# Low halves of q and k made by GpSimd from a float32 copy, in an attention and mixture-of-experts kernel

## The chip, the cores and the metric

One core of one Trainium2 chip runs the whole program. The metric is the device time in microseconds. The engines are TensorE (PE; its weight loads PEld), VectorE (DVE), ScalarE (ACT), GpSimd (POOL) and SyncE (SP), which issues most transfers. Matmul results lie in PSUM banks of 128 x 512 float32; the rest lies in SBUF.

## The reference

```python
# x: (16, 512, 256); 16 heads of 16; 8 experts of 512, two for each token
qkv = layernorm(x) @ W_attn + b_attn
q, k = rope(q), rope(k)                  # angles by head index
att  = softmax(causal(q @ k.T / 4))
x    = x + (att @ v) @ W_proj + b_proj
xf   = layernorm(x)
w    = top2(softmax((layernorm(xf) * ln_scale + ln_bias) @ gate_w.T))   # renormalised
x    = x + swiglu(xf, sWg, sWu, sWd) + sum_e w[:, e] * swiglu(xf, Wg[e], Wu[e], Wd[e])
```

## The kernel before

The program has an attention stage (to about 860 us), then the shared expert with the routing, then the routed experts. The change touches the attention stage alone.

Attention works on 16 batches of 512 tokens. A batch is a pass of `body(b, ...)`, and each engine runs its own copy of it: four groups `g` of four heads, and in each group five units `s`. A place (g, s) is called a slot here. In each slot TensorE makes the scores of one unit (`scores`, L1675, with the mask L1695), VectorE takes their row maxima (`row_max`), and TensorE may write the next scores only when the maxima are taken. Three slots into the next group the scores are made again with the row maxima subtracted (`shifted`, L1723), ScalarE takes the exponential (`exponentials`, L884), GpSimd clears what is above the diagonal (`select`, L702), and TensorE multiplies with v (`mix`, L1749). The maxima reach the operand as rows: `maxima` transposes them on TensorE (L1709, s = 0), ScalarE copies them to `m_row` (L893, s = 1), SyncE moves four rows into `q_op` (`load_shift`, L480, s = 2), and `shifted` of unit 0 (s = 3) waits for them.

All other work is placed by hand: constants name the slot of each step, and every engine does its steps in order of the slots. Beside batch b the projections of batch b + 1 are made, and the output projection and residual of batch b - 1. Float32 precision comes from pairs of halves: three products of a high and a low part stand for one (`products`, L1615).

q and k of the next batch are four blocks `i` of 128 x 512 (0 and 1: q and k of the first eight heads; 2 and 3: of the others). `project_qk(n, i)` writes each into the one bank `ps_q`. Then two engines read the bank:

```python
nc.scalar.activation(qkh[:, i, :], src[:], ACT.Identity, bias=bcol[:, i:i + 1])   # qk_high, L861
nc.vector.scalar_tensor_tensor(out=qkl[:, i, :], in0=src[:], scalar=bcol[:, i:i + 1],
                               in1=qkh[:, i, :], op0=ALU.add, op1=ALU.subtract)   # qk_low, L1077
```

Both results are float16. TensorE uses `ps_q` also for the transposes of the normalised input (`transpose_xn`, L1606) and for v (`project_v`), and it waits for `qkl_done` before three of these: `project_v` of j = 1 in slot (2,1), `project_qk` of i = 3 in (3,1), and the first `transpose_xn` in (0,1) of the next pass.

SyncE stores the halves to memory (`store_qk`, L458) and loads them back in the order of the heads, with high or low parts stacked (`load_qk`, L472, 12 transfers for each j). For j = 0 (blocks 0 and 1) store and first loads are in slot (2,3), and the loads go on to (3,3); for j = 1 the store is in (0,2) of the next pass. SyncE does all of this in one order, with `load_shift`, the loads of x, and `store_half` (L511, L512), which stores the residual rows. A wait of SyncE holds up all that is behind it.

GpSimd adds the bias of the output projection to the residual (`X_BIAS`, L723): one piece in (1,4), three in (3,2).

Of the kernel before, what the change touches and what calls it, by code (L numbers as in the profile page):

```python
# [16 lines left out]
P = 128  # L17
# [27 lines left out]
def build(nc, x, w_attn, b_attn, w_proj, b_proj, ln_scale, ln_bias, gate_w, Wg, Wu, Wd, sWg, sWu, sWd, rope, out):  # L45
# [41 lines left out]
    with ExitStack() as ctx:  # L87
# [9 lines left out]
        def sem(name):  # L97
# [57 lines left out]
        xh = sb_a("xh", [P, 2, T], F32R)  # L155
        xl = sb_a("xl", [P, 2, T], F32R)
        qkh = sb_a("qkh", [P, 4, T], F16)
        qkl = sb_a("qkl", [P, 4, T], F16)
# [89 lines left out]
                 "pool_const attn_w qk_topped biascols scales_done "  # L248
                 "xn_done shift_done xnT_in xh_done xl_done qk_in qkh_done qkl_done v_in v_done "
                 "s_in max_done m_in m_done mrow_in t_in exp_done sel_done pv_in o_done "  # L250
# [26 lines left out]
        XN_T, XN_HIGH, XN_LOW = ((0, 1), (0, 2)), ((0, 1), (0, 2)), ((0, 1), (0, 3))  # L277
        QK, QK_HIGH = ((0, 4), (1, 4), (2, 4), (3, 1)), ((1, 0), (2, 0), (3, 0), (3, 4))
        QK_LOW = ((1, 0), (2, 0), (3, 0), (0, 1))
        V_PROJ, V_PROJ_B, VALUES = ((1, 2), (2, 1)), ((1, 3), (2, 1)), ((1, 3), (2, 3))  # L280
# [6 lines left out]
        PROJ, PROJ_B = ((3, 3), (1, 1)), ((3, 4), (1, 1))  # L287
        X_BIAS = ((1, 4), (3, 2), (3, 2), (3, 2))
        X1, X1_STATS, X1_VARIANCE = ((3, 4), (1, 1)), ((0, 0), (1, 2)), ((0, 4), (2, 4))
# [349 lines left out]
        def _(pool):  # L639
# [42 lines left out]
            input_rstd(1)  # L682

            def residual_rstd(bp, j):
                pool.wait_ge(S["varb_done"], 2 * bp + j + 1)
                pool.sem_inc(S["pool_passed"], 1)
                nc.gpsimd.tensor_tensor(rstdb[:], mvb[:, :, 1], neghalf[:, 0:2],
                                        ALU.pow).then_inc(S["rstdb_done"], 1)
# [17 lines left out]
            def body(b, par, cur, prev, prev2, nxt, nxt2):  # L706
                for g in range(NG):
                    G = 4 * b + g
                    has1 = (cur or g < 1) and (prev or g >= 1)
                    has2 = (cur or g < 2) and (prev or g >= 2)  # L710
                    for s in range(UN):
                        if s >= LAG - UN and has1:
                            select(G - 1, s + UN - LAG, (g - 1) % 2)
                        elif s < LAG - UN and has2:
                            select(G - 2, s + 2 * UN - LAG, g % 2)
                        if prev:
                            for t in range(NT):
# [120 lines left out]
        def _(act):  # L838
# [16 lines left out]

            def qk_high(n, i, src=ps_q):

                act.wait_ge(S["qk_in"], 4 * n + i + 1)
                if some(32 * n):
                    act.wait_ge(qk_stored[i // 2], 32 * n)  # L860
                nc.scalar.activation(qkh[:, i, :], src[:], ACT.Identity,  # L861
                                     bias=bcol[:, i:i + 1]).then_inc(S["qkh_done"], 1)

            def prologue():
# [6 lines left out]
                for i in range(4):  # L871
                    qk_high(0, i, QK_BANK[i])
                for t in range(NT):
# [30 lines left out]
            def body(b, par, cur, prev, prev2, nxt, nxt2):  # L904
                for g in range(NG):
# [3 lines left out]
                    for s in range(UN):  # L909
                        for i in range(4):  # L910
                            if cur and prev and (g, s) == QK_HIGH[i] and QK_HIGH[i] < QK[i]:
                                qk_high(b, i)
                        if s == M_ROWS and has1:
# [16 lines left out]
                        if nxt:  # L930
# [3 lines left out]
                            for i in range(4):  # L934
                                if (g, s) == QK_HIGH[i] and QK_HIGH[i] >= QK[i]:
                                    qk_high(b + 1, i)
                        for j, bp in heads_here((g, s), Y_OUT, b, prev, prev2):
# [103 lines left out]
        def _(dve):  # L1041
# [32 lines left out]

            def qk_low(n, i, src=ps_q):
                dve.wait_ge(S["qkh_done"], 4 * n + i + 1)
                nc.vector.scalar_tensor_tensor(out=qkl[:, i, :], in0=src[:], scalar=bcol[:, i:i + 1],  # L1077
                                               in1=qkh[:, i, :], op0=ALU.add,
                                               op1=ALU.subtract).then_inc(S["qkl_done"], 1)
# [59 lines left out]
            def prologue_qkv():  # L1139
# [3 lines left out]
                for i in range(2):  # L1143
                    qk_low(0, i, QK_BANK[i])
                for j in range(2):
                    values(0, 0, j, V_BANK[j])
                for i in range(2, 4):
                    qk_low(0, i, QK_BANK[i])
                stats(1, 1, 0)
# [120 lines left out]
            def body(b, par, cur, prev, prev2, nxt, nxt2):  # L1270
                for g in range(NG):
                    G = 4 * b + g
                    for s in range(UN):
                        for i in range(4):
                            if cur and prev and (g, s) == QK_LOW[i] and QK_LOW[i] < QK[i]:
                                qk_low(b, i)
                        if cur:
                            row_max(G, g, s)
                        if nxt:
                            for c in range(2):  # L1280
                                if (g, s) == XN_LOW[c]:
                                    xn_low(b + 1, c)
                            for i in range(4):
                                if (g, s) == QK_LOW[i] and QK_LOW[i] >= QK[i]:
                                    qk_low(b + 1, i)
                            for j in range(2):
# [308 lines left out]
        def _(pe):  # L1595
            def transpose_xn(n, c, out=None):

                pe.wait_ge(S["xn_done"], n + 1)
                if out is None:
# [3 lines left out]
                    else:  # L1603
                        pe.wait_ge(S["qkl_done"], 4 * n)
                for t in range(NT):
# [13 lines left out]
            def project_qk(n, i, out=None):  # L1619
# [439 lines left out]
```

## Time and profile before

| | us |
|---|---|
| median of 3 runs | 1797.29 (1796.71 to 1798.85) |
| profiled execution | 1802.63 |
| its span | 1800.9 |
| PE busy | 1636.0 |
| DVE busy | 1169.6 |
| ACT busy | 874.3 |
| POOL busy | 780.0 |
| PE, DVE, ACT, POOL busy in 120 to 760 | 608.91, 556.14, 429.24, 238.63 |

Busy times are those of the profiled execution. Ends of matmuls are modelled: one matmul's time overlaps the start of the next, so that stalls of TensorE are better read from starts than from idle time. An engine's share over the whole span mixes stages with different limits; the last row is the attention stage in its steady part.

### The profile page before, as it was taken

Reading aid. Unit: us, or ns where it says so; the run is one execution under the profiler, and the core shown is the slowest. Engines: PE = TensorE matmul, PEld = TensorE weight load, DVE = VectorE, ACT = ScalarE, POOL = GpSimd, SP = SyncE. Lnnn points to the kernel's source line nnn. Section 1 sums busy time; section 2 is a strip of 40 time slices with the busy share of each in tenths; the row PEclk is TensorE's granted clock in tenths of the full one; section 3 lists DMA queues with packets and bytes.
Section 4 is the critical chain, followed back from the end, with each engine's and each line's share of the span. In section 5 each row is a group of like instructions: output and inputs, shape, how many; then the busy total and the mean of one; then the engine's idle time right before and its main releaser. Section 6 shows DMA issues by size and latency. Waiting matters only on the chain.

```text
span 1800.9 us, 45470 instructions
## 1 busy us (share of the span) xinstructions
PE 1636.0 (91%) x15505; PEld 1132.7 (63%) x15507; DVE 1169.6 (65%) x2062; ACT 874.3 (49%) x1273; POOL 780.0 (43%) x1005
## 2 busy tenths in 40 slices
PE   2689999999999999984798999989999999999996
PEld 2345555555555555432575566669999999999985
DVE  5568888888888888874358777874434444443442
ACT  1266666666666666552333222544444444444442
POOL 1023333333333333332200676725666666666652
PEclk9799999999999999987899999999999999999998
DMA  1322333333333333211536553223434333333432
GB/s 58 106 84 83 107 106 107 106 99 101 104 106 107 107 99 96 91 54 43 187 124 185 171 164 88 83 89 54 68 59 66 62 62 66 61 64 61 65 60 25
DMA packets 168709, 163.37 MB, mean 91 GB/s; under 512 B 29682, under 2 KB 159218, under 8 KB 168563
## 3 DMA queue, kind: packets, MB, share of 16 engines
q1 hardware_dynamic: 138354, 125.66, 22.8%
q0 software_dynamic: 30208, 35.81, 12.4%
q8 instruction: 86, 1.41, 0.3%
q14 instruction: 61, 0.49, 0.1%
HBM read 100.82 MB, written 60.30 MB: 89 GB/s over the span
## 4 chain that ended last, share of the span: by engine, by line
PE 68%; DVE 12%; issue 7%; DMA 5%; SPq 4%; ACT 3%; POOL 1%; DVEq 0%; POOLq 0%; ACTq 0%
PE bank L1615 21%; PE pair_s L1980 10%; PE pair_s L1615 7%; PE bank L1980 5%; PE pair_t L1980 5%; PE bank L1749 4%; PE pair_s L1675 3%; SPq L480 2%; PE pair_t L1723 2%; DVE mx L1165 2%; PE pair_t L1969 2%; ACT qkh L861 2%; SPq L472 1%; DMA q_op<-m_row 1%; PE bank L1765 1%
## 5 line engine op out<-in xcount | busy, mean ns | idle before, releaser
L884 ACT ACTIVATE prob<-pair_t 128x1024 f32<-128x1024 f32 x320 | 327.4, 1023 | 243.0 <-PE pair_t L1723 238.3
L702 POOL TENSOR_SCALAR_AFFINE_SELECT prob<-prob 128x256 f32<-128x256 f32 (+1 forms) x448 | 196.8, 453 | 478.0 <-ACT prob L884 466.4
L818 POOL DMA_INDIRECT out_x<-ysb,tok_rows x136 | 218.2, 1605 | 196.2 <-ACT ysb L1025 146.3
L1573 DVE SCALAR_TENSOR_TENSOR early<-pair_s,h_s,sg 128x512 f32<-128x512 f32 (+1 forms) x72 | 51.9, 721 | 249.0 <-PE pair_s L1980 249.0
L780 POOL DMA_INDIRECT tok_d<-tok_w,dest_i x128 | 126.6, 989 | 160.2 <-DVE dest_i L1424 121.5
L1980 PE MATMUL pair_s<-xt,wbuf 128*128 128x256 f16 (+1 forms) x1728 | 193.9, 267 | 1.9 <-DVE xt L1564 1.9
L1615 PE MATMUL bank<-wbuf,early 128*128 x1632 | 190.2, 273 | 0.9 <-ACT ysb L1025 0.8
L1749 PE MATMUL bank<-prob,v_op 128*32 128x512 f32 (+3 forms) x2048 | 181.5, 450 | 2.0 <-POOL prob L702 1.7
L1016 ACT CAST early<-early 128x512 f16<-128x512 f32 (+1 forms) x144 | 85.6, 594 | 196.6 <-DVE early L1573 196.6
L1615 PE MATMUL pair_s<-wsh,xt 128*128 128x512 f16 x768 | 179.2, 382 | 0.0
L1980 PEld LDWEIGHTS pair_s<-xt,wbuf 128*128 x1728 | 163.0, 98 | 22.3 <-issue 2.3
L1165 DVE TENSOR_REDUCE mx<-pair_s 128x2 f32<-128x1024 f32 x128 | 155.9, 1218 | 25.8 <-PE pair_s L1695 25.1
L799 POOL DMA_INDIRECT xrow<-xhl_d,tok_rows x136 | 136.5, 1003 | 74.3 <-issue 37.8
L1615 PEld LDWEIGHTS bank<-wbuf,early 128*128 128x128 f16 x1632 | 155.8, 98 | 19.6 <-issue 1.5
L1675 PE MATMUL pair_s<-k_op,q_op 48*128 48x512 f16 (+3 forms) x1024 | 127.6, 307 | 35.6 <-DVE mx L1165 13.9
L1675 PEld LDWEIGHTS pair_s<-k_op,q_op 48*128 48x128 f16 x1024 | 34.8, 94 | 155.4 <-DVE mx L1165 79.0
L1168 DVE TENSOR_REDUCE mx<-pair_s 128x2 f32<-128x768 f32 x128 | 121.8, 952 | 16.4 <-PE pair_s L1695 15.2
L1579 DVE TENSOR_TENSOR early<-early 128x512 f16<-128x512 f32 (+1 forms) x144 | 95.3, 662 | 55.1 <-ACT early L1016 49.6
L1723 PE MATMUL pair_t<-q_op,k_op 49*128 49x512 f16 (+3 forms) x1024 | 123.9, 299 | 6.6 <-DMA q_op<-m_row 4.1
L1615 PEld LDWEIGHTS pair_s<-wsh,xt 128*128 128x128 f16 x768 | 74.5, 98 | 75.3 <-issue 1.7
L1025 ACT ACTIVATE ysb<-bank,row_w 128x256 f32<-128x256 f32 x136 | 64.4, 473 | 87.9 <-PE bank L1615 87.8
L1980 PE MATMUL bank<-xt,wbuf 128*128 128x256 f16 (+1 forms) x864 | 103.2, 267 | 0.0
(259 smaller groups left out, 3090.8 us busy)
## 6 DMA issues: line engine op xcount, KB each, us to landing
q_op<-qk_d SPq DMA_DIRECT2D x192, 64.0 KB, 2.4
k_op<-qk_d SPq DMA_DIRECT2D x192, 64.0 KB, 2.4
x_in<-in_L_attn_x SPq DMA_DIRECT2D x16, 512.0 KB, 4.2
qk_d<-qkh SPq DMA_DIRECT2D x32, 256.0 KB, 2.5
qk_d<-qkl SPq DMA_DIRECT2D x32, 256.0 KB, 2.7
xres<-in_L_attn_x SPq DMA_DIRECT2D x16, 512.0 KB, 4.7
x_d<-x SPq DMA_DIRECT2D x32, 256.0 KB, 2.2
xhl_d<-xhl SPq DMA_DIRECT2D x32, 256.0 KB, 2.5
```

The costliest lines, as they stand in the source:

```text
L702: last = nc.gpsimd.affine_select(out=v, in_=v, compare_op=ALU.is_ge, fill=0.0, base=0, pattern=[[0, v.shape[1]], [1, P]], channel_multipli ...
L780: pool.indirect_dma_start(out=tok_d, out_offset=bass.IndirectOffsetOnAxis(ap=dest_i[:, t, k:k + 1], axis=0), in_=tok_w[:, t, k, :], in_off ...
L799: pool.indirect_dma_start(out=xrow[:, k % GATHERED], out_offset=None, in_=xhl_d, in_offset=bass.IndirectOffsetOnAxis(ap=tok_rows[:, k, 0:1 ...
L818: pool.indirect_dma_start(out=out, out_offset=bass.IndirectOffsetOnAxis(ap=tok_rows[:, k, 0:1], axis=0), in_=ysb[:, k % ROWS_AHEAD], in_of ...
L884: nc.scalar.activation(prob[:, half, u].rearrange("p a n -> p (a n)"), pair_t[:].rearrange("p a n -> p (a n)"), ACT.Exp, scale=exp_by).the ...
L1165: last = nc.vector.tensor_reduce(dst[:, 3, 2 * u:2 * u + 2], pair_s[:], AX_X, ALU.max)
L1168: nc.vector.tensor_reduce(dst[:, 2, c:c + 2], pair_s[:, :, 0:384], AX_X, ALU.max)
L1615: last = nc.tensor.matmul(out, a, m, start=(i == 0), stop=(i == n - 1))
L1675: nc.tensor.matmul(ps_s[a][:, lo:lo + P * (q + 1)], q_op[64 * a:64 * a + KR, par, pair, P * q:P * (q + 1)], k_op[64 * a:64 * a + KR, par, ...
L1723: last = nc.tensor.matmul(ps_t[a][:, lo:lo + n], k_op[rows, par, pair, P * k:P * (k + 1)], q_op[rows, par, pair, P * k:], start=start, sto ...
L1749: last = nc.tensor.matmul(ps_o[32 * h:32 * h + 32, P * k:], v_op[:, vpar, k, GH * gg + h, :], pr[:, unit, h % 2, lo:lo + n], start=(piece ...
L1980: last = nc.tensor.matmul(out[:, w * k:w * k + w], wbuf[:, a], xt2[:, par, x, 0:w], start=(i == 0), stop=(i == 3 * CC - 1))
```

## The change

ScalarE takes each block from the bank once, as float32, into a buffer `qkf` of two places in SBUF (4 KB a partition). GpSimd then makes the high half by a copy and the low half by a subtraction, both from `qkf`. VectorE has no part in it any more, save in the prologue, where batch 0 is done as before. The bank is free when ScalarE is done (`qkf_done`), and TensorE waits for that. ScalarE waits for the low half of two blocks ago before it writes `qkf` again. ScalarE's slots are those of before; GpSimd does block 0 in (1,1) and (1,2), block 1 in (2,1) and (2,2), block 2 in (3,1) and (3,3), block 3 in (0,0) and (0,1) of the next pass. The store and load slots stay. Three of the pieces of X_BIAS move from (3,2) to (2,0), (2,3) and (2,4).

```diff
+        qkf = sb_a("qkf", [P, 2, T], F32)
-        QK, QK_HIGH = ((0, 4), (1, 4), (2, 4), (3, 1)), ((1, 0), (2, 0), (3, 0), (3, 4))
-        QK_LOW = ((1, 0), (2, 0), (3, 0), (0, 1))
+        QK, QK_ROWS = ((0, 4), (1, 4), (2, 4), (3, 1)), ((1, 0), (2, 0), (3, 0), (3, 4))
+        QK_HIGH, QK_LOW = ((1, 1), (2, 1), (3, 1), (0, 0)), ((1, 2), (2, 2), (3, 3), (0, 1))
-        X_BIAS = ((1, 4), (3, 2), (3, 2), (3, 2))
+        X_BIAS = ((1, 4), (2, 0), (2, 3), (2, 4))
...
# GpSimd
+            def qk_high(n, i):
+
+                pool.wait_ge(S["qkf_done"], 4 * n + i + 1)
+                if some(32 * n):
+                    pool.wait_ge(qk_stored[i // 2], 32 * n)
+                nc.gpsimd.tensor_copy(qkh[:, i, :], qkf[:, i % 2, :]).then_inc(S["qkh_done"], 1)
+
+            def qk_low(n, i):
+
+                pool.wait_ge(S["qkh_done"], 4 * (n - 1) + i + 1)
+                nc.gpsimd.tensor_tensor(qkl[:, i, :], qkf[:, i % 2, :], qkh[:, i, :], ALU.subtract
+                                        ).then_inc(S["qkl_done"], 1)
...
+                        for i in range(4):
+                            for at, half in ((QK_HIGH[i], qk_high), (QK_LOW[i], qk_low)):
+                                if (g, s) == at and at < QK[i] and cur and prev:
+                                    half(b, i)
+                                elif (g, s) == at and at >= QK[i] and nxt:
+                                    half(b + 1, i)
...
# ScalarE
-            def qk_high(n, i, src=ps_q):
+            def qk_rows(n, i, src=ps_q):
 
                 act.wait_ge(S["qk_in"], 4 * n + i + 1)
-                if some(32 * n):
-                    act.wait_ge(qk_stored[i // 2], 32 * n)
-                nc.scalar.activation(qkh[:, i, :], src[:], ACT.Identity,
-                                     bias=bcol[:, i:i + 1]).then_inc(S["qkh_done"], 1)
+                if 4 * n + i > 5:
+                    act.wait_ge(S["qkl_done"], 4 * n + i - 1)
+                nc.scalar.activation(qkf[:, i % 2, :], src[:], ACT.Identity,
+                                     bias=bcol[:, i:i + 1]).then_inc(S["qkf_done"], 1)
...
# VectorE: qk_low in the body is gone
-                            if cur and prev and (g, s) == QK_LOW[i] and QK_LOW[i] < QK[i]:
-                                qk_low(b, i)
...
# TensorE: transpose_xn, project_qk, project_v
-                        pe.wait_ge(S["qkl_done"], 4 * n)
+                        pe.wait_ge(S["qkl_done" if n == 1 else "qkf_done"], 4 * n)
...
-                    pe.wait_ge(S["qkl_done"], 4 * n + i)
+                    pe.wait_ge(S["qkf_done"], 4 * n + i)
...
-                    pe.wait_ge(S["qkl_done"], 4 * n + j + 1)
+                    pe.wait_ge(S["qkf_done"], 4 * n + j + 1)
```

## Rows read from the trace of the kernel before

**Rows 1.** Windows: length; busy (count) of PE, PEld, DVE, ACT, POOL; clock; DMA; GB/s
```profile
120.00:760.00 640.00, 608.91 (x6157) 330.66 (x6156) 556.14 (x1027) 429.24 (x572) 238.63 (x480) 1.00 0.33 100
```

**Rows 2.** Waits of PE, 120 to 760 us: total, times, longest
```profile
PE bank L1615 <- DVE qkl L1077: 9.9, 28, 0.4
...
PE pair_t L1723 <- DMA q_op<-m_row: 3.1, 5, 1.1
```

**Rows 3.** Timeline of PE, slots (2,0) and (2,1): start, length, line
```profile
362.88 0.38 PE L1723 MATMUL pair_t<-q_op,k_op 49*128 49x384 f16 x4
363.19 0.60 PE L1709 MATMUL bank<-ident,mx 128*4 128x128 f32 x4
...
365.01 0.38 PE L1723 MATMUL pair_t<-q_op,k_op 49*128 49x384 f16 x4
365.75 0.39 PE L1615 MATMUL bank<-wah,xh 128*128 128x256 f32 x1 [0.35 <-DVE qkl L1077]
```

**Rows 4.** Timeline of PE, slot (3,1) and slot (0,1) of the next pass
```profile
376.48 0.38 PE L1723 MATMUL pair_t<-q_op,k_op 49*128 49x384 f16 x4
377.21 0.50 PE L1615 MATMUL bank<-xh,wah 128*128 128x512 f32 x1 [0.35 <-DVE qkl L1077]
...
434.01 0.38 PE L1723 MATMUL pair_t<-q_op,k_op 49*128 49x384 f16 x4
434.64 0.63 PE L1606 MATMUL bank<-ident,xn 128*128 128x128 f32 x4 [0.25 <-DVE qkl L1077]
```

**Rows 5.** Timeline of SyncE's queue, three places
```profile
369.18 0.37 SPq L458 DMA_DIRECT2D qk_d<-qkh  x1
369.59 0.49 SPq L458 DMA_DIRECT2D qk_d<-qkl  x1
372.45 0.32 SPq L472 DMA_DIRECT2D q_op<-qk_d  x1
...
377.07 2.60 SPq L480 DMA_DIRECT2D q_op<-m_row  x4
...
391.16 0.47 SPq L458 DMA_DIRECT2D qk_d<-qkl  x1
393.67 0.32 SPq L472 DMA_DIRECT2D q_op<-qk_d  x1
...
423.98 2.40 SPq L480 DMA_DIRECT2D q_op<-m_row  x4
```

**Rows 6.** Timelines of ACT and DVE, slots (2,0) and (3,1)
```profile
364.23 0.68 ACT L861 ACTIVATE qkh<-bank,bcol 128x512 f16<-128x512 f32 x1
364.94 0.75 DVE L1077 SCALAR_TENSOR_TENSOR qkl<-bank,bcol,qkh 128x512 f16<-128x512 f32 x1 [0.63 <-ACT qkh L861]
...
376.26 0.57 ACT L893 ACTIVATE m_row<-bank 4x512 f16<-4x512 f32 x1
```

**Rows 7.** The chain that ended last, 400 to 446 us: start, length
```profile
415.54 4.58 DMA qk_d<-qkl
```

**Rows 8.** Timeline of PE, slot (3,3) of two batches
```profile
381.40 0.38 PE L1723 MATMUL pair_t<-q_op,k_op 49*128 49x512 f16 x2
...
427.58 0.39 PE L1723 MATMUL pair_t<-q_op,k_op 49*128 49x512 f16 x2
```

**Rows 9.** Groups of POOL by form, whole span: busy us, mean ns
```profile
L723 POOL TENSOR_TENSOR xres<-xres,bpb 128x256 f32<-128x256 f32 x64 | 45.3, 729 | 9.0 <-issue 8.9
L702 POOL TENSOR_SCALAR_AFFINE_SELECT prob<-prob 128x512 f32<-128x512 f32 x64 | 40.6, 634 | 119.7 <-ACT prob L884 119.7
...
L646 POOL CAST ident_h<-ident 128x128 f16<-128x128 f32 x1 | 0.3, 289 | 0.1
```

**Rows 10.** Timeline of POOL, slot (2,2)
```profile
369.44 0.63 POOL L702 TENSOR_SCALAR_AFFINE_SELECT prob<-prob 128x512 f32<-128x512 f32 x1 [2.05 <-ACT prob L884]
```

**Rows 11.** Timeline of DVE, L1227 in slots (2,0) and (3,3)
```profile
365.61 0.68 DVE L1227 SCALAR_TENSOR_TENSOR xhl<-xf,xhl 128x512 f16<-128x512 f32 x1
...
382.99 1.06 DVE L1227 SCALAR_TENSOR_TENSOR xhl<-xf,xhl 128x512 f16<-128x512 f32 x1
```

More of the change, by code:

```diff
@@ L248, in build @@
                  "pool_const attn_w qk_topped biascols scales_done "
-                 "xn_done shift_done xnT_in xh_done xl_done qk_in qkh_done qkl_done v_in v_done "
+                 "xn_done shift_done xnT_in xh_done xl_done qk_in qkf_done qkh_done qkl_done v_in v_done "
                  "s_in max_done m_in m_done mrow_in t_in exp_done sel_done pv_in o_done "
@@ L854, in xn_high, with first_high @@
                 nc.scalar.copy(xh[:, c, :], src[:]).then_inc(S["xh_done"], 1)
-            def qk_high(n, i, src=ps_q):
+            def qk_rows(n, i, src=ps_q):
                 act.wait_ge(S["qk_in"], 4 * n + i + 1)
-                if some(32 * n):
-                    act.wait_ge(qk_stored[i // 2], 32 * n)
-                nc.scalar.activation(qkh[:, i, :], src[:], ACT.Identity,
-                                     bias=bcol[:, i:i + 1]).then_inc(S["qkh_done"], 1)
+                if 4 * n + i > 5:
+                    act.wait_ge(S["qkl_done"], 4 * n + i - 1)
+                nc.scalar.activation(qkf[:, i % 2, :], src[:], ACT.Identity,
+                                     bias=bcol[:, i:i + 1]).then_inc(S["qkf_done"], 1)
+            def first_high(i):
+                act.wait_ge(S["qk_in"], i + 1)
+                nc.scalar.activation(qkh[:, i, :], QK_BANK[i][:], ACT.Identity,
+                                     bias=bcol[:, i:i + 1]).then_inc(S["qkf_done"], 1)
             def prologue():
@@ L871, in prologue @@
                 for i in range(4):
-                    qk_high(0, i, QK_BANK[i])
+                    first_high(i)
                 for t in range(NT):
@@ L910, in body @@
                         for i in range(4):
-                            if cur and prev and (g, s) == QK_HIGH[i] and QK_HIGH[i] < QK[i]:
-                                qk_high(b, i)
+                            if cur and prev and (g, s) == QK_ROWS[i] and QK_ROWS[i] < QK[i]:
+                                qk_rows(b, i)
                         if s == M_ROWS and has1:
@@ L934, in body @@
                             for i in range(4):
-                                if (g, s) == QK_HIGH[i] and QK_HIGH[i] >= QK[i]:
-                                    qk_high(b + 1, i)
+                                if (g, s) == QK_ROWS[i] and QK_ROWS[i] >= QK[i]:
+                                    qk_rows(b + 1, i)
                         for j, bp in heads_here((g, s), Y_OUT, b, prev, prev2):
@@ L1073, in xn_low, with first_low @@
                                         ALU.subtract).then_inc(S["xl_done"], 1)
-            def qk_low(n, i, src=ps_q):
-                dve.wait_ge(S["qkh_done"], 4 * n + i + 1)
-                nc.vector.scalar_tensor_tensor(out=qkl[:, i, :], in0=src[:], scalar=bcol[:, i:i + 1],
+            def first_low(i):
+                dve.wait_ge(S["qkf_done"], i + 1)
+                nc.vector.scalar_tensor_tensor(out=qkl[:, i, :], in0=QK_BANK[i][:], scalar=bcol[:, i:i + 1],
                                                in1=qkh[:, i, :], op0=ALU.add,
@@ L1143, in prologue_qkv @@
                 for i in range(2):
-                    qk_low(0, i, QK_BANK[i])
+                    first_low(i)
                 for j in range(2):
@@ L1147, in prologue_qkv @@
                 for i in range(2, 4):
-                    qk_low(0, i, QK_BANK[i])
+                    first_low(i)
                 stats(1, 1, 0)
@@ L1273, in body @@
                     for s in range(UN):
-                        for i in range(4):
-                            if cur and prev and (g, s) == QK_LOW[i] and QK_LOW[i] < QK[i]:
-                                qk_low(b, i)
                         if cur:
@@ L1282, in body @@
                                     xn_low(b + 1, c)
-                            for i in range(4):
-                                if (g, s) == QK_LOW[i] and QK_LOW[i] >= QK[i]:
-                                    qk_low(b + 1, i)
                             for j in range(2):
```

## The prediction

> **What bounds the kernel now.** I first read the busy time by stage. In the attention stage (120 to 760 us, nearly fourteen batches of 46.2 us) TensorE is busy 609 of 640 us at full granted clock, VectorE 556, ScalarE 429 and GpSimd 239 [rows 1]. So TensorE is the limit there, VectorE is close behind, and GpSimd has room. The change touches no instruction after this stage, so all of its effect must come from here.
>
> Next I asked who waits for the low halves `qkl`. Among TensorE's waits it comes first: 9.9 us ahead of products, 28 times [rows 2], and further times ahead of transposes. These idle times count from modelled ends, so I take the true stall from starts. In slot (2,0) the shifted products L1723 start at 362.88 and the following instruction at 363.19, a spacing of 0.31 us. In slot (2,1) the same products start at 365.01, yet L1615 (`project_v`) starts at 365.75, where 365.32 was possible: a stall of 0.43 us [rows 3]. By the same spacing the stall is 0.42 us in (3,1) and 0.32 us in (0,1) [rows 4]. The other hand-overs of the bank (L1622 for i of 1 and 2, `project_v` for j of 0) wait on something else or have slack. So a batch holds 1.17 us of TensorE stall that goes away if the bank is released earlier.
>
> Third, I followed the DMA queue of SyncE, because it carries the other end of `qkl`: store, read back, then the shift rows of the next group, all in one order. In the batch at 354 to 400 us the store of half 0 is issued at 369.18 and 369.59, the loads start at 372.45, eight of them must be issued, and the shift rows of slot (3,2) go out at 377.07 [rows 5]. ScalarE had them ready at 376.83 (376.26 + 0.57) [rows 6]. So SyncE is late by 0.2 us already. In the batch after, the store takes 4.58 us to land, the shift rows go out only at 423.98, and TensorE starts L1723 of slot (3,3) at 427.58, which is 3.60 us later [rows 5, 7, 8]. That 3.6 us (three issues ahead, the fourth, its landing) is what an issue of L480 needs until TensorE may go on. In the first batch 377.07 + 3.6 = 380.7, and TensorE came at 381.40 [rows 8]: 0.7 us of slack. This path through SyncE is the one to watch. Today it isn't gated by `qkl` at all: the low half of i = 1 was done at 365.69 (364.94 + 0.75) [rows 6], 3.5 us before its store.
>
> **The change, part by part.**
>
> *ScalarE.* `qk_rows` replaces `qk_high` in the same slots, with the same input and bias, and float32 out. An activation of 128x512 took 0.68 us [rows 6]; I take the same. Its new wait (two blocks back in the ring `qkf`) is on a low half that GpSimd makes at least three slots earlier. Cost: nothing.
>
> *Release of the bank.* TensorE now waits for ScalarE's end, 364.91 in slot (2,0), instead of VectorE's, 365.69 [rows 6]. It is at the wait at 365.32, so all of the 0.43 us goes, and so do 0.42 in (3,1) and 0.32 in (0,1).
>
> *VectorE* loses 60 instructions of 0.75 us, 45 us in all, and its waits for ScalarE before them. Its row maximum then follows the scores sooner. It cannot add to the TensorE gain beyond these slots, because the stretches between them are filled by TensorE's own work; in (0,1) the chain scores, row maximum, scores then becomes as long as TensorE's, so I count 0.2 to 0.3 there instead of 0.32.
>
> *GpSimd* gets 60 copies and 60 subtractions of 128x512. The copy: a cast of 128x128 took 0.289 and a one-input select of 128x512 took 0.634 [rows 9]. I take 0.63. The subtraction has two inputs, and the nearest row is L723, 128x256 in 0.729 [rows 9]. The two one-input rows give (634 - 289)/384 = 0.90 ns an element and 0.17 us that is fixed. With the fixed part counted once, 512 columns come to 0.17 + 2 x 0.555 = 1.28 us. Bounds: 0.95 (only the one-input slope on top of 0.729), and 1.46 (twice 0.729). In sum 60 x 1.91 = 115 us on an engine that is idle 401 us in this stretch. Each piece stands behind the select of its slot and before the next select is ready: in (2,2) the select ends at 370.07 (369.44 + 0.63) [rows 10]. No select that TensorE waits for is queued behind a long piece; if one were, `mix` would be late.
>
> The skill's page "GPSIMD Engine Reference", section "Performance versus the Vector engine", gives 4497 ns for a two-input add of 2048 columns and tells one to keep elementwise work on VectorE. By the slope from L723 to that figure the subtraction would be 1.27 us, an estimate from that page; the sum would not change.
>
> *X_BIAS.* Three adds of 0.73 us move from (3,2) to (2,0), (2,3) and (2,4), each into a gap of GpSimd of over 1.3 us. Their reader is the residual of (3,4) or later. Nothing.
>
> *The store.* Here is the price. `store_qk` for half 0 waits for the low half of i = 1, which now comes behind the select of slot (2,2), itself behind the exponential of that slot. TensorE's gain in (2,1) pulls that select 0.43 us ahead. The low half is then ready at 370.07 - 0.43 + 1.28 + 0.1 (hand-over) = 371.02, and the store goes out then instead of at 369.18: 1.84 us late. Part comes back in the landing. Today this store is issued 0.6 us behind the two stores of `store_half` and lands after 2.86 us (369.59 to 372.45) or after 4.58 [rows 5, 7]. The store of half 1, with no such neighbour, landed after 2.51 us (391.16 to 393.67) [rows 5]. Issued 1.8 us later, half 0 should be like that one.
>
>  - Usual batch: loads start at 371.43 + 2.5 = 373.9 instead of 372.45, shift rows at 378.5, L1723 of (3,3) at 382.1 instead of 381.40: **0.7 us late**, the gains of (2,1) and (3,1) already in.
>  - Batch with a slow landing: loads at 0.4 us earlier than today, and L1723 **0.4 us early** instead of 0.85 us early.
>
> The same working for each of the thirteen batches between 184 and 740 us gives from -1.0 to +1.4 us each, +3.1 us together (landing 2.6 us). So SyncE takes back about all that TensorE won in (2,1) and (3,1). What stays is the gain of (0,1), which lies behind (3,3): 14 x 0.25 = 3.5 us. Sum: +3.1 (+3.3 for fourteen) - 3.5, that is **0 us**.
>
> Half 1 has the same change in (0,1): its store comes some 1.4 us later, but the shift rows of (1,2) have about 1.0 us of slack behind the loads and TensorE another 1.4. Nothing.
>
> The profiled execution took 1802.6 us (span 1800.9), the median of the runs is 1797.3; the sum is a difference, so I put it on the median: **1797 us**. A measurement of this kernel can tell about 0.2%, 3.6 us, from no change.
>
> **Rivals.**
>
> 1. *The queue does not bind (faster).* If the store's delay is absorbed, because the subtraction comes nearer 0.95 us and landings nearer 2.3, the three stalls all go: 1.1 us a batch, 15 us, 1782 us. Half of this is likelier than all: 1789. For it: in four of thirteen batches today's landing is over 4.3 us, and there the new one would be quicker. Against it: SyncE has no slack in most of the others. Chance 0.30.
>
> 2. *The later store lands no sooner (slower).* If slow landings come from the write itself and not from its neighbours, nothing of the delay comes back: 3.56 us (today's mean) instead of 2.6, times thirteen, is +12.5 us, 1810 us. It decides once the mean delay of L480 in (3,2) passes some 1.2 us against today. A subtraction of 1.46 us adds 0.2 x 14 = 2.5 us to it. For it: the queue is strictly in order and the 4.58 us landing wasn't seen to be caused by anything. Chance 0.25.
>
> 3. *The shared port (slower).* VectorE's L1227, with two inputs in SBUF, took 0.68 us alone and 1.06 us beside GpSimd's adds [rows 11]. If the 60 subtractions stretched by half, 0.6 us each, the store of half 0 would be late by that as well: 14 x 0.6 = 8 us, 1806 us. Against it: beside the new pieces in (2,1) and (2,2) VectorE mostly reads PSUM. Chance 0.05. The skill's "GPSIMD Engine Reference", section "Key points", says that the engines interfere on instructions of this kind; by that rule, the trace agrees.
>
> 4. *Forecast: about the same.* Chance 0.40.
>
> **How the numbers follow.** The forecast's own range is +-3.6 us (1793 to 1801). The range for 8 in 10 runs from half of rival 1 a little beyond to the whole of rival 2: 1786 to 1811. Faster by over 0.2%: 0.30; within: 0.40; slower: 0.30 (rivals 2 and 3).
>
> **What the new profile would show.** The three waits of TensorE for `qkl` are gone and none for `qkf` takes their place. GpSimd: copies near 0.63 us, subtractions near 1.28. In SyncE's queue the store of half 0 is issued about 1.3 us after the end of the select of (2,2), lands in about 2.5 us, and L480 of (3,2) goes out 1.5 to 2 us after its row is ready. TensorE's wait for `m_row`, 3.1 us in this stretch today [rows 2], grows to some 15 us. The prediction is wrong if that wait stays small, or if it grows beyond 20 us. It would also be wrong by its mechanism if `mix` began to wait for selects, or if the adds of X_BIAS delayed one.

## The result, and the profile after

The changed kernel is slower: median 1814.24 us of five runs (1807.59 to 1819.18), against 1797.29 (1796.71 to 1799.71) for the kernel before. The ratio of the runs is 1.0074, with a 95% interval from 1.0056 to 1.0093; the two medians alone make 1.0094, since the runs of the changed kernel lie far apart. So the loss is 13 us by the ratio and 17 us by the medians. Two things stand out besides the sign. The five runs lie 11.6 us apart, where those of before lie 3.0 us apart. And the profiled execution, 1807.61 us with a span of 1805.9, is at the lower end of them, so its trace shows the change at its mildest.

The page of the changed kernel, its busy times and the chain of work that ended last (shares of the span; SPq is SyncE's queue, DMA the transfers themselves):

```profile
PE 1630.3 (90%) x15505; PEld 1130.4 (63%) x15507; DVE 1127.1 (62%) x2002; ACT 874.3 (48%) x1273; POOL 880.4 (49%) x1125
...
PE 65%; SPq 9%; DMA 9%; DVE 5%; issue 5%; ACT 3%; POOL 3%; POOLq 0%; DVEq 0%; ACTq 0%
```

In the chain SyncE's queue has now 9% and transfers 9%, where the kernel before had 4% and 5%; VectorE has fallen from 12% to 5%. The steady part of the attention stage and TensorE's waits in it (line numbers have moved by 20 for TensorE: L1743 are the shifted products, L1769 `mix`, L1695 the scores, L1635 the products, L1804 the output projection):

```profile
120.00:760.00 640.00, 601.69 (x6094) 327.88 (x6094) 510.35 (x960) 424.46 (x565) 328.21 (x585) 0.99 0.32 99
```

```profile
PE pair_t L1743 <- DMA q_op<-m_row: 20.6, 17, 2.7
PE pair_s L1695 <- DMA k_op<-qk_d: 3.2, 7, 0.8
PE bank L1769 <- POOL prob L716: 3.1, 14, 0.2
PE bank L1635 <- DVE v_op L1113: 2.7, 14, 0.2
```

The waits for `qkl` are gone [rows 2], VectorE has 46 us less to do, GpSimd 90 us more. In their place TensorE waits 20.6 us for the shift rows, where it waited 3.1. Two smaller waits are new or longer: `mix` waits 14 times for a select, which it did nowhere in this stretch before, and the wait for `k_op` is 3.2 us, where the kernel before had:

```profile
PE pair_s L1675 <- DMA k_op<-qk_d: 0.6, 2, 0.3
```

And SyncE, which never waited for `qkl` in this stretch before, waits for it 27 times (its queue's own waits):

```profile
SPq L466 <- DMA qk_d<-qkl: 61.4, 27, 3.8
SPq L454 <- POOL qkl L695: 38.1, 27, 2.8
```

One batch shows the whole of it. TensorE in slots (2,1) and (3,1), GpSimd in (2,2), SyncE's queue, and TensorE in (3,3), the timelines of the changed kernel:

```profile
366.34 0.38 PE L1743 MATMUL pair_t<-q_op,k_op 49*128 49x384 f16 x4
366.65 0.39 PE L1635 MATMUL bank<-wah,xh 128*128 128x256 f32 x1
...
377.28 0.38 PE L1743 MATMUL pair_t<-q_op,k_op 49*128 49x384 f16 x4
377.60 0.50 PE L1635 MATMUL bank<-xh,wah 128*128 128x512 f32 x1
```

```profile
370.24 0.63 POOL L716 TENSOR_SCALAR_AFFINE_SELECT prob<-prob 128x512 f32<-128x512 f32 x1 [0.95 <-ACT prob L910]
370.84 1.16 POOL L695 TENSOR_TENSOR qkl<-qkf,qkh 128x512 f16<-128x512 f32 x1
```

```profile
372.16 0.37 SPq L459 DMA_DIRECT2D qk_d<-qkh  x1
372.57 0.47 SPq L459 DMA_DIRECT2D qk_d<-qkl  x1
375.07 0.32 SPq L473 DMA_DIRECT2D q_op<-qk_d  x1
...
379.53 2.60 SPq L481 DMA_DIRECT2D q_op<-m_row  x4
```

```profile
383.33 0.39 PE L1743 MATMUL pair_t<-q_op,k_op 49*128 49x512 f16 x2 [1.38 <-DMA q_op<-m_row]
```

From the shifted products to the next instruction it is 0.31 and 0.32 us, the unstalled spacing of [rows 3]: both stalls at the bank are gone. GpSimd's subtraction ends at 372.00, SyncE issues the store at 372.16, the shift rows go out at 379.53, and TensorE stands idle for 1.38 us at L1743 of (3,3). There was no such wait in [rows 8].

To compare all batches I take the thirteen steady ones (those of the prediction's sum) and count each time from the maxima of slot (2,0) of its batch, L1709 before and L1729 after. Means in us, worked out from the timelines. A landing is counted from the issue of the store of `qkl` to the issue of the first load behind it; "behind" is from L1743 of (3,3) to the maxima of (0,0), which is 4.61 when nothing disturbs it. The ratio stands beside, with its interval.

| kernel | store of `qkl` issued | its landing | shift rows of (3,2) out | L1743 of (3,3) | behind | ratio |
|---|---|---|---|---|---|---|
| before | 6.60 | 3.56 | 14.27 | 18.45 | 4.61 | 1 |
| changed | 8.06 | 2.98 | 15.04 | 19.03 | 4.73 | 1.0074 (1.0056 to 1.0093) |
| changed again | 8.07 | 2.99 | 15.05 | 19.14 | 5.41 | 1.0072 (1.0051 to 1.0094) |
| one slot earlier | 6.58 | 3.57 | 14.17 | 18.07 | 4.84 | 0.9979 (0.9967 to 0.9991) |
| both earlier | 6.72 | 3.42 | 14.22 | 18.08 | 4.62 | 0.9968 (0.9955 to 0.9981) |
| late store alone | 8.59 | 2.74 | 15.29 | 19.19 | 4.62 | 1.0064 (1.0042 to 1.0086) |
| wait filled | 8.07 | 2.86 | 14.98 | 19.26 | 4.61 | 1.0074 (1.0061 to 1.0087) |
| row stores apart | 5.37 | 3.02 | 13.76 | 18.21 | 4.75 | 1.0003 (0.9992 to 1.0015) |
| earlier and apart | 5.94 | 2.99 | 13.45 | 17.59 | 4.73 | 0.9939 (0.9924 to 0.9954) |
| load alone | 6.57 | 3.51 | 14.34 | 18.49 | 4.60 | 1.0016 (1.0006 to 1.0026) |
| loads later | 8.06 | 2.93 | 14.02 | 17.97 | 4.85 | 0.9987 (0.9973 to 1.0000) |
| all three | 5.96 | 3.03 | 13.28 | 17.47 | 5.63 | 0.9990 (0.9977 to 1.0004) |
| early halves, late loads | 6.70 | 3.45 | 13.51 | 17.69 | 4.78 | 0.9929 (0.9909 to 0.9948) |
| before, late loads | 6.69 | 3.39 | 13.89 | 18.28 | 4.66 | 0.9989 (0.9975 to 1.0003) |

The first ten experiments ran on two other chips, where the kernel before took 1963 to 1964 us. The time is lost in the expert stage: between 900 and 1300 us TensorE is busy for 251 of 400 us at a granted clock of 0.82, where the trace of before has 382 us at 1.00. What it waits for there I didn't look into. So of these experiments I use ratios, and the attention stage alone of their traces, which has a mean clock of 0.99 or 1.00 between 120 and 760 us in all of them. The same loss in us makes an 8% smaller ratio there. Of before there is only the trace from the first chip. The window of the changed kernel on such a chip:

```profile
900.00:1300.00 400.00, 250.94 (x2064) 166.79 (x2061) 174.63 (x336) 77.82 (x114) 123.11 (x129) 0.82 0.30 92
```

### The profile page after: what moved, and what is told of

It reads as the page before. It is cut to its first block, busy times and chain, and to the rows that moved or that the text cites. A ratio compares the mean times of both kernels' runs of the same rounds, so it can differ in the third digit from the quotient of the medians.

```text
span 1805.9 us, 45588 instructions
## 1 busy us (share of the span) xinstructions
PE 1630.3 (90%) x15505; PEld 1130.4 (63%) x15507; DVE 1127.1 (62%) x2002; ACT 874.3 (48%) x1273; POOL 880.4 (49%) x1125
## 4 chain that ended last, share of the span: by engine, by line
PE 65%; SPq 9%; DMA 9%; DVE 5%; issue 5%; ACT 3%; POOL 3%; POOLq 0%; DVEq 0%; ACTq 0%
PE bank L1635 19%; PE pair_s L2000 10%; PE pair_s L1635 7%; SPq L473 5%; PE bank L2000 5%; PE pair_t L2000 5%; PE bank L1769 4%; DMA qk_d<-qkl 3%; SPq L481 3%; PE pair_s L1695 3%; PE bank L1804 2%; PE pair_t L1743 2%; DMA k_op<-qk_d 2%; ACT prob L910 2%; DMA q_op<-m_row 2%
## 5 line engine op out<-in xcount | busy, mean ns | idle before, releaser
L1635 PE MATMUL bank<-wbuf,early 128*128 x1632 | 190.3, 273 | 0.9 <-ACT ysb L1051 0.8
L1769 PE MATMUL bank<-prob,v_op 128*32 128x512 f32 (+3 forms) x2048 | 180.0, 447 | 5.5 <-POOL prob L716 5.4
L1635 PE MATMUL pair_s<-wsh,xt 128*128 128x512 f16 x768 | 178.6, 381 | 0.0
L1635 PEld LDWEIGHTS bank<-wbuf,early 128*128 128x128 f16 x1632 | 156.1, 98 | 19.3 <-issue 1.3
L1695 PE MATMUL pair_s<-k_op,q_op 48*128 48x512 f16 (+3 forms) x1024 | 127.7, 308 | 34.9 <-DMA k_op<-qk_d 12.7
L1743 PE MATMUL pair_t<-q_op,k_op 49*128 49x512 f16 (+3 forms) x1024 | 124.0, 299 | 29.2 <-DMA q_op<-m_row 27.1
L1695 PEld LDWEIGHTS pair_s<-k_op,q_op 48*128 48x128 f16 x1024 | 34.6, 94 | 153.8 <-DVE mx L1191 69.6
L1635 PEld LDWEIGHTS pair_s<-wsh,xt 128*128 128x128 f16 x768 | 74.5, 98 | 75.0 <-issue 1.1
```

Of the source, the lines that this page charges most:

```text
L1635: last = nc.tensor.matmul(out, a, m, start=(i == 0), stop=(i == n - 1))
L1695: nc.tensor.matmul(ps_s[a][:, lo:lo + P * (q + 1)], q_op[64 * a:64 * a + KR, par, pair, P * q:P * (q + 1)], k_op[64 * a:64 * a + KR, par, ...
L1743: last = nc.tensor.matmul(ps_t[a][:, lo:lo + n], k_op[rows, par, pair, P * k:P * (k + 1)], q_op[rows, par, pair, P * k:], start=start, sto ...
L1769: last = nc.tensor.matmul(ps_o[32 * h:32 * h + 32, P * k:], v_op[:, vpar, k, GH * gg + h, :], pr[:, unit, h % 2, lo:lo + n], start=(piece ...
```

## The experiments

**The changed kernel again**, unedited.

> The changed kernel once more, unedited, to have it on the same chip as the others and to see its spread. In its profile a wait of TensorE for the shift rows in slot (3,3), 1.5 us a batch, is followed in one place by a granted clock of 0.81. If both belong to the change, its runs spread again from about 1807 to 1819 us, the slower ones at a lower mean clock (0.968 to 0.971 against 0.974 to 0.978). If the spread was an accident of one chip, they agree within 3 us.

Ratio 1.0072; six runs from 1971.99 to 1986.97, 15 us apart, where 23 runs of before lie 10.3 us apart. The spread comes again. The profiled execution is here the slowest of the six (1986.97). The main difference to the first profile is the column "behind": it is 6.2 to 7.5 us in five of the thirteen batches. TensorE in two slots of one of them:

```profile
247.92 0.61 PE L1743 MATMUL pair_t<-q_op,k_op 49*128 49x512 f16 x2 [2.37 <-DMA q_op<-m_row]
...
249.47 2.08 PE L1804 MATMUL bank<-wp,y_t 128*128 128x256 f32 x4
251.48 0.61 PE L1695 MATMUL pair_s<-k_op,q_op 48*128 48x256 f16 x4
```

After a wait of 2.37 us the same instructions take about twice their time (L1804 2.08 us instead of 1.13, the scores 0.61 instead of 0.39): the lower level of the clock. In the five batches such a stall costs its own length and then another 1.5 to 2.9 us.

**The low half one slot earlier.** The edit to the changed kernel:

```diff
-        QK_HIGH, QK_LOW = ((1, 1), (2, 1), (3, 1), (0, 0)), ((1, 2), (2, 2), (3, 3), (0, 1))
+        QK_HIGH, QK_LOW = ((1, 1), (2, 0), (3, 1), (0, 0)), ((1, 2), (2, 1), (3, 3), (0, 1))
-        X_BIAS = ((1, 4), (2, 0), (2, 3), (2, 4))
+        X_BIAS = ((1, 4), (2, 2), (2, 3), (2, 4))
```

> The changed kernel with the halves of block 1 made one slot earlier: copy in (2,0), subtraction in (2,1), and the add of X_BIAS of (2,0) moved to (2,2). The subtraction is then done before SyncE comes to the store of half 0. Theory A (the late store delays the shift rows of (3,2)): store back at +6.4 us behind the maxima of (2,0) instead of +8.0, the wait of TensorE for m_row falls from 20.6 us to under 6, time 1790 to 1796 us. Rival B (GpSimd's load or the shared port is what costs): the work on GpSimd is the same, so the time stays at 1805 to 1815. Rival C (the gain at the bank is not real): no wait is left, but the time is that of the kernel before, 1797.

Ratio 0.9979: from 0.7% slower to 0.2% faster by moving two instructions of GpSimd by a slot (and one add of X_BIAS out of their way). The store is back at 6.58 us. Rival B is out, since the same work is done by the same engine, and so is C, whose ratio would be 1. The wait for the shift rows was to fall under 6 us and fell only by half, though:

```profile
PE pair_t L1743 <- DMA q_op<-m_row: 10.7, 15, 2.5
```

With the store where it always was, TensorE, now 0.85 us ahead of its old time at (3,3), runs into SyncE's queue. L1743 is at 18.07, 0.38 us earlier than before instead of 0.85. SyncE's queue alone takes more than half of the gain back. One batch of this trace has the lower clock too, behind a wait of 2.50 us, which makes the 4.84 in "behind".

**Both halves earlier:** block 3 as well, copy in (3,4), subtraction in (0,0).

```diff
+        QK_HIGH, QK_LOW = ((1, 1), (2, 0), (3, 1), (3, 4)), ((1, 2), (2, 1), (3, 3), (0, 0))
```

> As the one before, and block 3 too: copy in (3,4), subtraction in (0,0) in place of (0,0) and (0,1). Theory A: half 1 had slack of some 2.4 us, so little more than e1: 0 to 3 us faster than it, by the group (1,0) to (2,0), which grew in some batches of the changed kernel, and by the select of (0,1), which TensorE now waits for. If the wait for the select of (0,1) is set by the exponential and not by the new pieces, the group (0,0) to (1,0) stays at 10.57 us.

Ratio 0.9968, 3.0 us less than the run before at the median, at the edge of what was expected and with intervals that overlap. The group (0,0) to (1,0) stays at 10.58 us: the wait for the select isn't due to the new pieces. The group from the maxima of (1,0) to those of (2,0) falls from 12.83 to 12.56 us, and it was 12.59 before: the late store of half 1 costs there (more below).

**The late store alone**, in the kernel before: GpSimd makes one spare subtraction in (2,2), and the store of half 0 waits for it.

```diff
+                if j == 0 and n:
+                    sp.wait_ge(S["late_done"], n)
...
+                        if nxt and (g, s) == (2, 2):
+                            nc.gpsimd.tensor_tensor(spare_h[:, 1], spare_f[:], spare_h[:, 0], ALU.subtract
+                                                    ).then_inc(S["late_done"], 1)
```

> The kernel before, with one thing of the change alone: GpSimd makes one more subtraction of 128x512 in slot (2,2) of each batch, on spare data, and the store of half 0 waits for it. ScalarE, VectorE and TensorE work as before. Theory A: the store is late by 2.2 us and L1723 of (3,3) by 1.0 to 1.5 us a batch, none of it paid back: 1812 to 1825 us, with drops of the clock. Rival B (GpSimd's other pieces cost): a twelfth of the load, so under 1800.

Ratio 1.0064. The store goes out at 8.59, L1723 of (3,3) comes at 19.19, 0.74 us later than before instead of 1.0 to 1.5, and no clock drop is seen in the thirteen batches of this profile. The time expected, 1812 us or more (a ratio of 1.008), was missed with it. With bank, ScalarE and VectorE as they were, this wait by itself makes the kernel about as slow as the change does, with a store that is 0.5 us later still. So the late store is shown from both sides: taken away, the loss goes; put in alone, it comes.

**The wait filled**, in the changed kernel: six matmuls on the identity ahead of the wait for the shift rows.

```diff
+                if u == 0 and gg == 2:
+                    for _ in range(6):
+                        nc.tensor.matmul(ps_t[0][:].rearrange("p (s n) -> p s n", n=P), ident_h[:],
+                                         ident_h[:].unsqueeze(1).broadcast_to([P, 4, P]), start=True, stop=True)
```

> The changed kernel with six matmuls of 512 columns on the identity, into the bank that the shifted products write next, put between the scores of (3,3) and TensorE's wait for the shift rows (with the wait for the exponential moved ahead of them); they change no result. They fill some 1.3 us of the wait and add no wait. Theory A1 (in the changed kernel a fifth to a third of the stalls is followed by some microseconds at the lower clock, 1.6 to 2.9 us lost each time): maxima of (0,0) behind L1743 of (3,3) at 4.61 us in all batches, instead of up to 7.5, and 3 to 8 us less than the changed kernel. Rival: the stalls are all of it; time as the changed kernel, +-2 us.

"Behind" is 4.61 us in all thirteen batches: no drop is left, as A1 has it. But the ratio is 1.0074, no better. The filling costs where the wait would have been shorter (L1743 at 19.26 instead of 19.14), and the time of A1, 3 to 8 us less, is missed. The five runs lie 4.8 us apart (1975.62 to 1980.46) instead of 15. So the drops are likely what spreads the runs of the changed kernel, but it isn't shown: the runs are few, and the six of the late store alone lie 12 us apart (1970.52 to 1982.50) with no drop in the batches of its profile. How much of the median the drops make isn't settled either.

**The row stores apart**, in the kernel before, and **earlier halves with row stores apart**, in the changed kernel. Both have this edit, the second has that of both halves earlier too:

```diff
-        XRES, ROWS_OUT = (1, 2), ((2, 2), (3, 4))
+        XRES, ROWS_OUT = (1, 2), ((3, 3), (3, 4))
```

> The kernel before with the two stores of store_half 0 moved from slot (2,2) to (3,3), so that they no longer stand ahead of the store of half 0. If those neighbours made that store land slowly (my prediction's assumption), it lands in 2.5 us in all batches instead of 2.9 to 5.0, and goes out 1.2 us sooner. If the slow landings come from elsewhere, 4.5 us landings remain in the same batches. In both cases the shift rows of (3,2) are on time more often; TensorE has 0.7 us of slack there, so 0 to 5 us faster.

> The changed kernel with both of: halves of blocks 1 and 3 made earlier (as in the run of both earlier), and the stores of store_half 0 in (3,3). Theory A (SyncE's queue is what takes the gain at the bank back): with the queue freed, L1743 of (3,3) comes at 17.6 us behind the maxima of (2,0), limited by TensorE, against 18.45 before; 0.8 us a batch, ratio 0.992 to 0.995. Rival: something else pins the group (the exponentials and selects, as in (0,2)): ratio 0.997, as with both earlier alone.

Ratios 1.0003 and 0.9939. In the kernel before, the edit brings the shift rows out at 13.76 instead of 14.27 and gains nothing, since TensorE comes at 18.2 in any case. The landing becomes 2.5 us in nine of thirteen batches, but 4.4 to 4.9 us remain in three. So my assumption on the landing was half right: the neighbours explain 2.9 against 2.5, not the long ones. In the changed kernel, as theory A has it, the same edit is worth 0.3%: L1743 of (3,3) is at 17.24 us in about half of the batches, 0.95 us ahead of the usual 18.19 of before. The full gain at the bank is there once SyncE's queue is out of its way, and TensorE waits for the shift rows only this long:

```profile
PE pair_t L1743 <- DMA q_op<-m_row: 3.8, 6, 1.3
```

**The load alone**, in the kernel before: copies and subtractions on spare data in the slots of the change, X_BIAS moved as there, nobody waiting.

```diff
+            def spare_high(n, i):
+                nc.gpsimd.tensor_copy(spare_h[:], spare_f[:]).then_inc(S["spare_done"], 1)
...
+            def spare_low(n, i):
+                nc.gpsimd.tensor_tensor(spare_l[:], spare_f[:], spare_h[:], ALU.subtract
+                                        ).then_inc(S["spare_done"], 1)
```

> The kernel before, with all of GpSimd's new work beside it: copy and subtraction of 128x512 for each block, in the slots of the change and on spare data, and X_BIAS moved as in the change; nobody waits for them. Theory A (only the place of the low half in SyncE's chain costs): ratio 0.998 to 1.002. Rival 3 (load on GpSimd, shared port): slower by 0.3% or more, with longer VectorE instructions of two SBUF inputs.

Ratio 1.0016: a small loss, within A's band at the point value and with an interval clear of 1. One place of it shows in the trace. VectorE's `input_shift` in (2,1), a four-column instruction with its inputs in SBUF, takes 383 ns on average instead of 163. The average mixes two cases: in eleven of the thirteen it starts 0.2 us after GpSimd's copy, takes 0.41 us and ends within 0.02 us of the copy's end; of the other two one starts late in the copy and takes 0.15, one has a select beside it and takes 0.31. The row maximum behind it is late, and TensorE waits for it (VectorE by form, then TensorE's waits):

```profile
L1089 DVE SCALAR_TENSOR_TENSOR shift<-mv,rstd 128x4 f32<-128x4 f32 x13 | 5.0, 383 | 0.0
```

```profile
PE pair_s L1697 <- DVE mx L1187: 5.8, 14, 2.1
```

In the kernel before that wait was 2.1 us, once. In the changed kernel it is 1.1 us, once: VectorE without `qk_low` has room for it. So rival 3 is real in kind and small, 0.16% with VectorE as full as before, and no part of the loss of the changed kernel is seen to come from it. That these waits make up the 0.16% isn't shown: the thirteen batches take 600.8 us in this trace and 601.0 in that of before, and the profiled execution was the fastest of its twelve.

**The loads one slot later**, in the changed kernel. The store stays late, and only the order in SyncE's queue changes: six loads instead of eight ahead of the shift rows. Then the same with all other edits, with the early halves alone, and in the kernel before as the control:

```diff
-        QK_STORE, QK_LOAD = ((2, 3), (0, 2)), ((2, 3), (0, 3))
+        QK_STORE, QK_LOAD = ((2, 3), (0, 2)), ((2, 4), (0, 3))
```

> The changed kernel with the loads of half 0 begun one slot later, in (2,4): the store stays late, but six loads instead of eight stand in SyncE's queue ahead of the shift rows of (3,2), and six instead of four behind them. Theory A (order in SyncE's queue): shift rows out at about 14.1 us behind the maxima of (2,0) instead of 15.0, L1743 of (3,3) at 18.1 instead of 19.0, fewer drops of the clock; ratio 0.998 to 1.003. The operands of the next pass land no later than before. Rival: the landing of the store itself decides, whatever the order; ratio 1.007.

> The kernel of earlier halves and stores apart, with the loads of half 0 begun in (2,4) too. Theory A: in e6 six waits for the shift rows are left, 3.8 us, and three late maxima; most of the first go: ratio 0.990 to 0.994. If TensorE is the limit there already, 0.994 as without it.

> The changed kernel with halves of blocks 1 and 3 made earlier and the loads of half 0 begun in (2,4), the stores of store_half 0 left in (2,2). In the run of all three those stores, in (3,3), stood ahead of the last loads of the operand, and TensorE waited 17.7 us for k_op at (0,0). Theory A: here that wait is under 6 us and the wait for m_row under 6 us, ratio 0.990 to 0.995. If the last loads are late without those stores too, 0.997 to 1.000.

> The kernel before with the loads of half 0 begun in (2,4), nothing else: the control for the changed kernel with that edit. TensorE had 0.7 us of slack at (3,3) in most batches, so only the batches of slow landings can gain: ratio 0.998 to 1.000. If it is 0.992 or less, that edit is a gain by itself and says nothing of the late store.

With a store as late as in the changed kernel (8.06) the shift rows go out at 14.02 and the ratio is 0.9987: an order of issues pays for the whole loss. The control gives 0.9989 (0.9975 to 1.0003), so the edit itself is worth 0.1% at most, not clear of nothing; the rest is the late store made harmless. With all three edits the expectation was missed: 0.9990. "Behind" rises to 5.63, and the wait tells why:

```profile
PE pair_s L1695 <- DMA k_op<-qk_d: 17.7, 15, 2.3
PE pair_t L1743 <- DMA q_op<-m_row: 3.3, 6, 1.3
```

The row stores now stand in (3,3) ahead of the last two loads, and the scores of (0,0) wait for these. Without the row stores there, it has the lowest ratio of all, 0.9929 (1787.96 us against 1799.46 for before on the same chip), though not clear of the 0.9939 of earlier and apart; both waits are under 6 us, as expected:

```profile
PE pair_t L1743 <- DMA q_op<-m_row: 5.5, 8, 1.3
PE pair_s L1695 <- DMA k_op<-qk_d: 3.9, 6, 1.2
```

## Why the prediction was wrong

The forecast was 1797 us, as before, and the measured median is 1814. The main mechanism, the gated store of half 0, was the one forecast; three terms of the sum were wrong or put at nothing, and the clock was not in it.

*Right.* The three stalls at the bank went to zero (0.31 and 0.32 us of spacing in (2,1) and (3,1), and the same in (0,1)). The subtraction took 1.16 us where I had 1.28, the copy 0.61 where I had 0.63:

```profile
L695 POOL TENSOR_TENSOR qkl<-qkf,qkh 128x512 f16<-128x512 f32 x54 | 62.6, 1160 | 0.0
L690 POOL CAST qkh<-qkf 128x512 f16<-128x512 f32 x55 | 33.5, 609 | 0.0
```

The Trainium skill's "GPSIMD Engine Reference" ("Performance versus the Vector engine") had given 1.27 by my estimate; the measurement decides, 1.16. The store went out 1.64 us late in the usual batch (6.40 to 8.04 us) where I had 1.84, and the shift rows 1.7 to 2.9 us behind their row in ten of the thirteen batches, where I had 1.5 to 2 for the usual one. TensorE's wait for them was to grow to some 15 us and grew to 20.6. Two of the signs that the prediction named for being wrong came: a wait beyond 20 us, and `mix` waiting for selects.

*The first step that failed: "lands in about 2.5 us", 2.6 in the sum.* The landing fell from 3.56 to 2.98 us, not to 2.6. Four stores of the thirteen still took 3.2 to 4.2 us, and the run with the row stores apart shows that such landings come without neighbours too. In some batches the shift rows themselves took up to 1.8 us more than the 3.6 I had for them. Together, L1743 of (3,3) came 0.58 us later than before in the mean, where the sum had 3.1 / 13 = 0.24. That is 0.34 us a batch, 5 us in fourteen.

*The second: "What stays is the gain of (0,1)".* It does not stay. The stall there went, and 0.2 us later TensorE waits for a select:

```profile
391.58 0.38 PE L1743 MATMUL pair_t<-q_op,k_op 49*128 49x256 f16 x4
392.19 1.07 PE L1769 MATMUL bank<-prob,v_op 128*32 128x384 f32 x16 [0.22 <-POOL prob L716]
```

From the shifted products to `mix` in (0,2) it is 0.61 us, where 0.32 is the spacing in (2,2) (368.62 to 368.94). Its select follows the exponential of (0,1), which the change leaves where it was. The group from (0,0) to (1,0) is 10.57 us in nearly every batch of both kernels, and it stayed so when the new pieces were moved out of (0,1). I had looked at the row maxima and TensorE's own work for what else pins this slot, not at the way through ScalarE and GpSimd. The term was 3.5 us.

*The third: half 1, put at "Nothing".* Its store goes out at 5.90 us behind the maxima of (0,0) instead of 4.97, lands in 3.17 us instead of 2.65, and five of TensorE's seven waits for `k_op` stand in front of the scores of (2,0). The group from the maxima of (1,0) to those of (2,0) takes 12.81 us instead of 12.59, 3 us in fourteen; half of it comes from the last of the thirteen batches (13.48 us instead of 11.96). In the five traces with this store as late the group takes 12.67 to 12.88 us, in the other nine 12.49 to 12.72.

The first two give 0 + 5 + 3.5, about 8.5 us, and in the profiled execution the last maxima of (0,0) come at 812.2 us instead of 803.9, 8.2 us later. That the two agree is luck. The thirteen batches, from maxima of (2,0) to maxima of (2,0), take 612.6 us instead of 601.0, 11.7 more: 7.5 up to L1743 of (3,3), 1.6 behind it (the clock, below), 2.9 with half 1, and -0.3 in the group between. Ahead of them and behind them the changed kernel gains 3.4 us. The rest of that span, which the change doesn't touch, was 3.2 us shorter.

*Missing altogether: what a stall does to the clock.* In one of the thirteen batches of the first profile a wait of 1.75 us is followed by the lower level. The windows and TensorE's timeline in it:

```profile
520.00:526.00 6.00, 4.25 (x53) 1.93 (x51) 4.61 (x10) 2.56 (x5) 2.01 (x4) 0.97 0.24 69
526.00:534.00 8.00, 7.80 (x60) 4.03 (x57) 4.43 (x6) 5.16 (x8) 3.26 (x6) 0.81 0.49 148
534.00:540.00 6.00, 5.68 (x71) 3.05 (x70) 5.33 (x10) 4.35 (x7) 2.89 (x5) 1.00 0.27 88
```

```profile
525.07 0.39 PE L1743 MATMUL pair_t<-q_op,k_op 49*128 49x512 f16 x2 [1.75 <-DMA q_op<-m_row]
...
526.17 2.08 PE L1804 MATMUL bank<-wp,y_t 128*128 128x256 f32 x4
528.18 0.61 PE L1695 MATMUL pair_s<-k_op,q_op 48*128 48x256 f16 x4
...
529.26 1.13 PE L1804 MATMUL bank<-wp,y_t 128*128 128x256 f32 x4
```

The two L1804 are the same four matmuls, 2.08 and 1.13 us. Here it happened once, for 1.6 us; in the second profile, the slowest of its six runs, five times, for 10.4 us. That one has 21.5 us more in the thirteen batches than the trace of before: 8.9 up to L1743 of (3,3), 10.4 of the clock, 2.4 with half 1, and -0.2 in the group between. In the five timed runs the three slower ones (1814.2 to 1819.2) have a mean granted clock of 0.968 to 0.971, the two at 1807.6 one of 0.974 and 0.978. With the waits filled the spread went from 15 to 4.8 us. That the drops make much of the spread is thus likely, with the reserve said at the run with the wait filled. Their share in the median stays open, because filling the wait cost as much as it saved (615.1 us for the thirteen batches, between the 612.6 and the 622.5 of the two traces). The upper end of my range, 1811, was worked out from stalls alone.

*The rivals.* Rival 2 (the later store lands no sooner, 1810 us) is the nearest in its time, though not in its cause: the landing did shrink, by 0.58 of the 0.96 us. Rival 1, the queue that doesn't bind, is what the kernel can be made to do, but not as it was changed. Rival 3 costs 0.16% alone and nothing visible here.

The forecast weighed a gain that was sure (three short stalls) against a delay on a chain without slack. With the store gated at 8.04 us the best of the thirteen batches has its shift rows out at 14.27 and L1743 of (3,3) at 17.87 us, 0.3 us ahead of the usual 18.19 of before, though TensorE alone could be there at 17.24, as the run with the queue freed shows. All that goes slower than in the best batch is paid: four of the thirteen batches come 0.10 to 0.52 us earlier there than in the kernel before, nine come 0.26 to 1.65 us later. A gain at the bank is of use on such a chain only as far as the queue lets it.

## What to carry to other kernels

When work moves to another engine, follow its result as well as its source: here the bank was free 0.8 us sooner, but a store that had had 3.5 us of slack became gated, in an in-order queue that carried the next group's operand too. Before moving an instruction for good, move it by one slot, or move what stands behind it in the queue: one slot of GpSimd's table, or one slot of the loads, was worth 0.9% here, more than the 0.7% that the change itself cost. And look at the spread of the runs: a new stall in TensorE can cost its length and then the clock.

## What the runs showed of the hardware

- Right behind waits of TensorE from 1.75 to 2.62 us the granted clock fell to its lower level (1.2 of 2.4 GHz) for some microseconds in 6 of the 26 steady batches seen of the changed kernel; after others of 2.04 to 2.73 us it didn't. It isn't peculiar to the change: the kernel before has a drop too, between 122 and 126 us (0.63 and 0.52), behind a wait of 2.14 us for VectorE. The Trainium skill's "TensorE: Matmul & The Clock Gate" (Part 1) describes two levels, of which the lower follows idle time, and transitions that vary from run to run. The two traces agree in both, with one drop in the first and five in the second. The section ties the lower level to longer idle times than these waits; here the measurement decides.
- Stores of 256 KB to memory landed in 2.5 us in nine of thirteen batches with no other stores right ahead of them (2.9 us with such stores, in half of them), and in 4.3 to 5.1 us in some batches of both kinds (three of thirteen with none, four with).
- VectorE's four-column instruction took 0.41 us where it started 0.2 us behind the start of a GpSimd copy of 0.61 us, and ended with that copy; it took 0.15 us in twelve of the thirteen batches of the kernel before, which has no such copy.
